# Two stacked convolutions on one core: nine slots for x, and the second convolution's border products behind all its bands

## The reference

```
def _gn(v, G=32, eps=1e-05):           # mean and variance over 3 channels x 128 x 128, per image
    ...
x = x + _L0_conv_ref(_gn(x), w1, w3, w5, alpha)   # alpha0*g + alpha1*dw1(g) + alpha2*dw3(g) + alpha3*dw5(g), depthwise
x = x + _L1_conv_ref(_gn(x), w, b)                # one 3x3 kernel for all channels, plus a bias
```

## Time and profile before

| | us |
|---|---|
| median of 3 runs | 429.32 |
| lowest, highest | 427.31, 429.94 |
| the profiled execution | 432.64 |
| its span | 430.8 |
| busy: PE, DVE, ACT, POOL | 318.5, 318.1, 304.1, 262.3 |

### The profile page before, as it was taken

One profiled execution on the slowest core, in us unless ns is written; L12 is line 12 of the kernel. 1 busy time (PEld: TensorE's weight loads), 2 busy tenths in 40 slices (PEclk: granted clock), 3 DMA queues, 4 the chain that ended last, 5 costly groups with the idle time before them and its releaser, 6 DMA issues.

```text
span 430.8 us, 12547 instructions
## 1 busy us (share of the span) xinstructions
PE 318.5 (74%) x5206; PEld 276.8 (64%) x5206; DVE 318.1 (74%) x688; ACT 304.1 (71%) x372; POOL 262.3 (61%) x206
## 2 busy tenths in 40 slices
PE   2491586754986998679894998499848989898440
PEld 2361273643986798459883897389836989897220
DVE  7861899971886998399929994889649996779620
ACT  1407257089999699939995899759993999977320
POOL 6405055058788578827885588738882788865601
PEclk9997596995999899969996999889998999999685
DMA  6689488201687769676986788676868514731965
GB/s 151 169 174 204 129 188 169 73 3 41 159 200 164 199 177 210 158 189 202 199 194 171 198 184 202 161 214 173 189 163 223 145 41 118 201 97 28 264 173 146
DMA packets 112829, 69.40 MB, mean 161 GB/s; under 512 B 4540, under 2 KB 109892, under 8 KB 112772
## 3 DMA queue, kind: packets, MB, share of 16 engines
q1 hardware_dynamic: 106088, 65.31, 60.5%
q10 hardware_dynamic: 6684, 3.29, 3.3%
HBM read 41.10 MB, written 27.48 MB: 159 GB/s over the span
## 4 chain that ended last, share of the span: by engine, by line
DVE 33%; DMA 21%; SPq 13%; ACT 13%; PE 9%; issue 4%; ACTq 2%; POOL 2%; POOLq 0%; DVEq 0%
DVE xt L697 15%; DVE stats L641 13%; DMA xt<-in_x_dram 10%; PE ps L377 8%; DMA edge_scratch<-gnX 6%; ACT gn_f L551 5%; SPq L236 5%; ACT gnX L552 4%; ACT cross L561 3%; SPq L216 3%; DMA edge_scratch<-gnY 2%; SPq L250 2%; POOL gnX L864 1%; SPq L263 1%; ACTq L244 1%
## 5 line engine op out<-in xcount | busy, mean ns | idle before, releaser
L377 PE MATMUL ps<-gnX,band 64*64 64x512 f16 x2880 | 181.6, 397 | 29.9 <-DVE xt L697 18.1
L377 PEld LDWEIGHTS ps<-gnX,band 64*64 64x64 f16 x2880 | 161.1, 188 | 46.6 <-issue 40.2
L697 DVE SCALAR_TENSOR_TENSOR xt<-ps,unscale,xt 128x512 f32<-128x512 f32 (+1 forms) x194 | 143.8, 747 | 22.9 <-PE ps L377 20.1
L641 DVE BATCH_NORM_STATS2 stats<-xt 128x6 f32<-128x384 f32 x256 | 120.9, 546 | 45.6 <-DMA xt<-in_x_dram 44.9
L377 PE MATMUL ps<-gnY,band 64*64 64x512 f16 x1728 | 116.8, 414 | 33.7 <-DVE xt L697 33.7
L864 POOL TENSOR_TENSOR gnX<-gn_f,gnX 128x768 f16<-128x768 f32 x60 | 92.7, 1545 | 60.7 <-ACT gnX L552 60.7
L377 PEld LDWEIGHTS ps<-gnY,band 64*64 64x64 f16 x1728 | 97.9, 190 | 49.1 <-ACT gnY L552 23.0
L551 ACT ACTIVATE gn_f<-xt,g_add,g_mul 128x768 f32<-128x768 f32 x120 | 122.1, 1017 | 4.9 <-DVE g_add L681 4.3
L864 POOL TENSOR_TENSOR gnY<-gn_f,gnY 128x768 f16<-128x768 f32 x60 | 92.7, 1545 | 31.0 <-ACT gnY L552 31.0
L561 ACT ACTIVATE cross<-ps,unscale 64x512 f32<-64x512 f32 x94 | 64.2, 683 | 51.0 <-PE ps L377 49.4
L873 POOL TENSOR_TENSOR xt<-xt,cross 128x512 f32<-128x512 f32 x47 | 61.7, 1315 | 57.3 <-ACT cross L561 57.2
(11 more groups left out here) (78 smaller groups left out, 97.9 us busy)
## 6 DMA issues: line engine op xcount, KB each, us to landing
out_dram<-xt SPq DMA_DIRECT2D x56, 384.0 KB, 4.8
xt<-in_x_dram SPq DMA_DIRECT2D x48, 384.0 KB, 6.4
band<-diag_scratch SPq DMA_DIRECT2D x48, 160.0 KB, 3.0
haloX<-edge_scratch SPq DMA_DIRECT2D x32, 123.4 KB
xt<-in_x_dram SPq DMA_DIRECT2D x20, 192.0 KB, 4.3
xt<-in_x_dram ACTq DMA_DIRECT2D x12, 192.0 KB, 6.0
out_dram<-xt SPq DMA_DIRECT2D x12, 192.0 KB, 4.0
haloX<-edge_scratch SPq DMA_DIRECT2D x32, 61.7 KB
```

Of the source, the lines that this page charges most:

```text
L377: mm = nc.tensor.matmul(ps[to, c, half, :], weights(rows, half), moving(rows, half), start=first, stop=last)
L641: st = nc.vector.bn_stats(stats[:, q_of(at, i) % 2, at, b, e, :], flat[:, SUB * e:SUB * (e + 1)])
L697: ev = nc.vector.scalar_tensor_tensor(out=here, in0=ps[frm, c, half, :].rearrange("h (b w) -> h b w", b=NB), scalar=unscale[rows, at:at + ...
```

## The change

`xt` gets nine slots of one unit. The channels of a unit are chosen so that two units that follow each other still lie side by side in DRAM; when they do in `xt` too (`joint`), one transfer per image and half moves both, as before. `in_and_out` now stores in odd periods and loads in even ones (the first pair in period 1). `cross` has two slots used in turn in place of one per channel. The weights of X's border products overlap in `halo_wX` (66 columns apart, not 128). TensorE does the bands of all three channels of Y ahead of its border products. The diff, cut to its core (renamed calls of the same meaning and semaphore counts are left out):

```diff
-    NX = 4
+    NX = 9
+    PRE = 4
...
-        halo_w = [sb("halo_wX", [P, NU * CG, 2, R], fp16), sb("halo_wY", [P, 2, R], fp16)]
+        halo_w = [sb("halo_wX", [P, NU * CG * (R + FAR[0]) + R - FAR[0]], fp16), sb("halo_wY", [P, 2, R], fp16)]
...
-        xt = sb("xt", [P, NX, NB, 2, CG, 2, W])
+        xt = sb("xt", [P, NB, NX, CG, 2, W])
...
-        cross = sb("cross", [P, NCROSS, NB, W])
+        cross = sb("cross", [P, 2, NB, W])
...
-            return 4 * CG * (i // 2) + 2 * CG * g + CG * (i % 2)
+            return C // 2 * g + CG * i
...
+        def joint(n):
+
+            return n % NX + 1 < NX
...
+            def stores_in(j):
+
+                if j < LAG + 1:
+                    return None
+                if j == LAG + 1 or j >= NU:
+                    return j - LAG - 1, 1
+                return (j - LAG - 2, 2) if j % 2 else None
+
+            def loads_in(j):
+
+                if j == 1:
+                    return PRE
+                return j + PRE if j % 2 == 0 and 2 <= j < NU - PRE else None
...
             def in_and_out(j, batches):
 
-                m = (j + 3) // 2 if j % 2 else j // 2 - LAG
                 for b in batches:
-                    if j % 2 and 2 <= m < NU // 2:
-                        if m >= NX:
-                            sp.wait_ge(stored[m % NX], 128 * (m // NX))
-                        load_pair(sp, m, b)
-                    elif j % 2 == 0 and m >= 0:
-                        unit_ready(2 * m + 1)
-                        store_pair(sp, m, b)
-                    elif j == PERIODS - 1:
-                        unit_ready(LAST - 1)
-                        store_unit(sp, LAST - 1, b)
+                    if stores_in(j) is not None:
+                        n, units = stores_in(j)
+                        unit_ready(n + units - 1)
+                        store(sp, n, b, units)
+                    n = loads_in(j)
+                    if n is not None:
+                        if n + 1 >= NX:
+                            sp.wait_ge(stored[b], 32 * stores_until(n + 1 - NX))
+                        if joint(n):
+                            load(sp, n, b, 2, x_in[n // 2 % 2])
+                        else:
+                            for k in range(n, n + 2):
+                                load(sp, k, b, 1, x_in[n // 2 % 2])
...
                 if i >= LAG:
                     conv(Y, i - LAG, 0, None, i + 2 if i == LAG or i == NU else None, 0, 5)
                     conv(Y, i - LAG, 1)
-                    if i - LAG < LAST:
-                        edge(Y, i - LAG, 0)
                     conv(Y, i - LAG, 2)
-                    if i - LAG == LAST:
-                        edge(Y, i - LAG, 0)
-                    edge(Y, i - LAG, 1)
-                    edge(Y, i - LAG, 2)
+                    for c in range(CG):
+                        edge(Y, i - LAG, c)
...
-                if i >= 1:
-                    act.wait_ge(cross_added, NCROSS * (i - 1) + min(c, NCROSS - 1) + 1)
+                k = crosses_before(i, c)
+                if k >= 2:
+                    act.wait_ge(cross_added, k - 1)
```

More of the change, by code:

```diff
@@ L133, in preact_conv_stack @@
         x_unit_in = [sem(f"x_unit_in{n}") for n in range(1, 4)]
-        x_in = [sem(f"x_in{r}") for r in range(NX)]
+        x_in = [sem(f"x_in{r}") for r in range(2)]
         band_in = [sem(f"band_in{p}") for p in range(2)]
-        stored = [sem(f"stored{r}") for r in range(NX)]
+        stored = [sem(f"stored{b}") for b in range(NB)]
         edges_landed = [sem(f"edges_landed{s}") for s in "XY"]
@@ L193, in crossed_to, with crosses_before @@
             return sum(crossed(n, c) for n in range(i + 1) for c in range(CG))
+        def crosses_before(i, c):
+            return crossed_to(i - 1) + sum(crossed(i, k) for k in range(c))
         def halo_landed(n):
@@ L239, in edges_in, with images, rows_of, loaded @@
                        .then_inc(halo_in[s][p], 16)
-        def load_unit(eng, n, b, done):
+        def images(t, n, g, b, units):
+            c = first_channel(n, g)
+            return t[b, c:c + units * CG, :, :].rearrange("c (e p) w -> p (c e) w", e=2)
+        def rows_of(n, g, b, units):
+            at = n % NX
+            return xt[HALVES[g], b, at:at + units, :, :, :].rearrange("p u c e w -> p (u c e) w")
+        def joint(n):
+            return n % NX + 1 < NX
+        def loaded(n):
+            return sum(128 if joint(k) else 256 for k in range(PRE, n + 1, 2) if (k - n) % 4 == 0)
+        def load(eng, n, b, units, done):
             for g in range(2):
[L243 to L247, removed]
+                eng.dma_start(rows_of(n, g, b, units), images(x, n, g, b, units)).then_inc(done, 16)
+        def store(eng, n, b, units):
             for g in range(2):
[L249 to L265, removed]
+                eng.dma_start(images(out, n, g, b, units), rows_of(n, g, b, units)).then_inc(stored[b], 16)
         @block.sync
@@ L276, in _ @@
             for b in range(2, NB):
-                load_unit(sp, 0, b, x_first_in[b])
+                load(sp, 0, b, 1, x_first_in[b])
             def save_runs(rows, to, done):
@@ L311, in _ @@
             for b in range(NB):
-                load_unit(sp, 1, b, x_unit_in[0])
+                load(sp, 1, b, 1, x_unit_in[0])
             edges_out(sp, X, 0)
@@ L323, in _ @@
             for b in range(NB):
-                load_unit(sp, 3, b, x_unit_in[2])
+                load(sp, 3, b, 1, x_unit_in[2])
             def unit_ready(n):
@@ L329, in unit_ready, with stores_until @@
                 sp.wait_ge(cross_added, crossed_to(n))
+            def stores_in(j):
[8 more added lines that the diff above has]
+                return j + PRE if j % 2 == 0 and 2 <= j < NU - PRE else None
+            def stores_until(n):
+                return sum(stores_in(j) is not None and sum(stores_in(j)) <= n + 1 for j in range(PERIODS))
             def in_and_out(j, batches):
[L333 removed]
                 for b in batches:
[L335 to L344 removed]
+                    if stores_in(j) is not None:
[11 more added lines that the diff above has]
+                                load(sp, k, b, 1, x_in[n // 2 % 2])
             for j in range(PERIODS):
@@ L364, in _ @@
             for b in (0, 1):
-                store_unit(sp, LAST, b)
-            for r in range(NX):
-                sp.wait_ge(stored[r], 256 if r < NX - 1 else 384)
+                store(sp, LAST, b, 1)
+            for b in range(NB):
+                sp.wait_ge(stored[b], 32 * (stores_until(LAST) + 1))
         @block.tensor
@@ L523, in _ @@
             for b in range(2):
-                load_unit(act, 0, b, x_first_in[b])
+                load(act, 0, b, 1, x_first_in[b])
             act.wait_ge(const_ready, 3)
@@ L582, in _ @@
             for b in range(NB):
-                load_unit(act, 2, b, x_unit_in[1])
+                load(act, 2, b, 1, x_unit_in[1])
             root(1)
@@ L613, in _ @@
             for b in (2, 3):
-                store_unit(act, LAST, b)
+                store(act, LAST, b, 1)
         @block.vector
@@ L869, in cross_add @@
             def cross_add(i, c):
-                pool.wait_ge(cross_out, crossed_to(i - 1) + sum(crossed(i, k) for k in range(c + 1)))
+                k = crosses_before(i, c)
+                pool.wait_ge(cross_out, k + 1)
                 here = x_of(i)[:, :, c, 1, :]
-                nc.gpsimd.tensor_tensor(here, here, cross[:, c, :, :], ALU.add).then_inc(cross_added, 1)
+                nc.gpsimd.tensor_tensor(here, here, cross[:, k % 2, :, :], ALU.add).then_inc(cross_added, 1)
             mid = diag[:, R - 1 - PAD:R + PAD, :][:, ::-1, :]
```

17 lines of the change are left out of this document (9 added, 8 removed).

## The result

The changed kernel takes **450.04 us** (median of 4, 447.00 to 452.16) against 428.31 us for the kernel before on the same chip. The ratio is 1.0503, with an interval of 1.0424 to 1.0583: 5% slower, where 425.6 us was forecast and 436 was the upper end of the range. The profiled execution took 452.16 us, its span is 450.4 us. Some executions of a kernel fall into a slower state, and the ratios here leave those out, so a ratio need not be the quotient of the two medians beside it.

The account below looks back on a forecast made before the run. SP's queue of loads, stores and border transfers was taken as the bound. −3.9 (body) − 1.2 (start) + 1.4 (end) = −3.7 us gave 428.9 in the profile's frame, 425.6 us as a median; range 414 to 436.

Parts of the forecast that it names:

- SP's length: SP's load and store halves 3 to 10: extra load issues add 1 us, four saves of diagonals 3 us.
- half 11: A half runs between two starts of SP's load-or-store block; this one was to start at 300.1, from 296.14.
- What bounds the kernel: Whole loop: SP's full queue sets the pace, 45.4 to 45.9 us a pair of halves; VectorE's stall is its visible end.
- rival 1: Whole loop: engines set the pace, all 34.7 us of VectorE's waits for x go; median 395 us, chance 0.07.
- The body: Loop up to unit 12's evacuation: waits for X's borders replace VectorE's 34.7 us stall, gaining only 3.9 us.
- relief by draining: Saves behind stores: the delay lets queued bytes drain, shortening the next block, so half of their 1.57 us each was taken.
- From unit 12 on: Late loop, no loads left: periods between evacuations were to be 19.25 us both before and after the change.
- TensorE's order: Y's border products behind all Y bands: taken to cost 0, other end +1.2 us for ScalarE's crossing in three late periods.
- The start: Zeroing of halo_wX ahead of VectorE's work on the kernels: 1.38 us in place of 2.62, so −1.2 us.
- The end: Eight stores ahead of unit 14's Y borders: +3.7 us, less 2.3 for faster landing with fewer queued bytes; together +1.4.
- Rival 3: SP's halves and the end: every added instruction counts, start gains nothing; slower, median 437 us, chance 0.20.
- None of the four: The rivals: engines set the pace (395 us, 0.07), added work hidden (418, 0.22), every instruction counts (437, 0.20), nothing (429, 0.10).

Follow-up runs that it names:

- run 5: Changed kernel with 98 unused columns at the end of halo_wX, so that xt starts on a multiple of 512 bytes: 421.13 us, 0.9803.
- run 4: Changed kernel with SP's saves of diagonals moved from store halves to load halves: 444.91 us, 1.0306.
- run 12: Changed kernel with xt aligned and saves in load halves, keeping its new TensorE order: 419.21 us, 0.9755.
- run 7: Changed kernel with xt aligned, saves in load halves and the old TensorE order: 416.22 us, 0.9712.
- run 2: Kernel before with only the new TensorE order, Y's border products behind the bands of all three channels: 435.64 us, 1.0109.
- run 3: Changed kernel with TensorE's old order of Y's border products: 449.66 us, 1.0412.
- run 8: As run 7, with the stores of units 11 and 12 behind the borders of Y of unit 14: 419.15 us, 0.9779.
- run 6: Kernel before with 320 unused bytes ahead of xt, which then starts 64 over a multiple of 256: 452.57 us, 1.0542.
- run 9: Kernel before with 256 unused bytes ahead of xt: 429.84 us, 0.9978.
- run 10: Kernel before with 128 unused bytes ahead of xt: 441.73 us, 1.0288.
- run 11: Kernel before with 320 unused bytes behind xt, so xt stays and the tiles behind it move: 430.31 us, 1.0024.

## Why the prediction was wrong

**The step that failed** is in "SP's length": the block of loads and borders takes 10.4 us "because of the bytes queued (205.24 to 215.68), and the bytes are the same". The bytes were the same and the packets weren't: 37.8 ns each in place of 33.9. The block itself grew only from 10.4 to 11.1 us, but the same assumption stands behind every other length and landing that the sum carried over. The change to halo_wX was priced by its memset alone (−1.2), but it also set where xt begins. I had asked what the smaller tile itself costs, and not what lies behind it. In numbers: 450.04 against 421.13 with xt aligned, and 452.57 against 429.42 in the kernel before. The misplacement costs 23 us there and nearly 29 here, which is more than the whole loss. In the sum, half 11 was due at 298.9 (300.1 less the start's 1.2) and came at 320.06, +21.2; from there to the start of half 15 (due at 374.2, which is 379.3 less 3.9 and 1.2; it came at 401.34) 6.0 us more were lost; the end gave back 3.9. Together 23.3, the distance of 450.4 from the forecast span of 427.1. Against the same kernel aligned (run 5) the changed one is 11.9 us late at half 5 (163.90 for 152.04) and 26.0 at half 11 (320.06 for 294.10).

**What bounds the kernel: right.** SP and its transfers make up 67% of the chain; in the middle SP waits for no engine to speak of; rival 1 (engines set the pace, 395 us) is out in every run. That fits a price of 11% on a packet and 5% on the time.

**The body, right once its packets are.** "Not −34.7" and the exchange of the stall for haloX waits hold in both versions: 36.8 us as changed, 24.3 us aligned. Evacuations in the middle came 23.8 to 27.3 us apart as changed, where 22 to 24 was forecast. With xt aligned, halves 5 to 11 take 142.06 us, 4.3 more than before, where saves and extra issues were put at 4.0. The split was off: of the 16 loads in half 4 no share falls in those halves, and three saves do, each at its full 1.6 us in a store half (runs 4 and 12); no relief by draining shows. Unit 12 is evacuated at 312.01 in run 5 (316.7 was forecast with the start), 17.9 us after half 11 began, where 17.8 was taken; in the changed kernel at 339.00, 18.9 after.

**From unit 12 on, wrong by little.** Periods were to be 19.25; as changed they are 21.5 (339.00 to 360.51) and then 20.9, 3.9 of the 6.0 us above. The last wait for haloX ends at 338.22, so slow packets aren't what stretches them: TensorE waits 3.0 us for VectorE in the two and is busy for 20.3 and 19.2 us, at a mean granted clock of 0.92 of full speed, a mix of its two levels, 2.4 and 1.2 GHz. Ahead of the first it had stood 5.4 us for haloX. In the kernel before, the last two such periods had a clock of 1.00, 2.4 GHz throughout, and 17.9 and 17.7 us of work (the one ahead of them, after a stall, took 19.15 at 0.91, with 15.8 us of work in it). Run 5 has 19.6 us at 1.00 and then 20.8 at 0.92; run 7 has 20.9 at 0.87, then 19.3 and 19.2 at 1.00. So these periods go with the granted clock, which the forecast took to stay as it was; why it fell where it did stays open.

**TensorE's order: wrong** in the kernel before: +1.1%, some 4.7 us, where 0 was taken with +1.2 as the other end (run 2). The path over ScalarE to SP's border write was missed. In the changed kernels it is hidden or too small to tell (runs 3 and 12).

**The start.** VectorE's rows of the changed kernel:

```profile
2.66 1.40 DVE L656 MEMSET halo_wX<- 128x1615 uint32 x1 [0.29 <-issue]
...
4.37 0.34 DVE L774 TENSOR_SCALAR kern<-k_w,k_alpha 97x25 f32<-97x25 f32 x1
...
42.67 3.78 DVE L666 BATCH_NORM_STATS2 stats<-xt 128x6 f32<-128x384 f32 x8 [9.30 <-DMA xt<-in_x_dram]
```

The memset takes 1.40 us (1.38 forecast) and the work on the kernels begins 1.4 us sooner (4.37; 5.74 in the trace before), so the test that I named, a start near 5.5, comes out in its favour. SP's save follows, 7.27 for 8.53. But the 9.30 us wait for unit 2's x stays as it was (9.03), and the gain is gone by SP's loads at 34.10 (33.12 before); half 1 begins at 57.10, 4.1 us later than before. With xt aligned the same row reads

```profile
33.93 3.78 DVE L666 BATCH_NORM_STATS2 stats<-xt 128x6 f32<-128x384 f32 x8 [0.36 <-DMA xt<-in_x_dram]
```

half 1 begins at 50.08 (52.98 before), and half 5 starts 6.3 us earlier than before, where 1.2 was forecast for all of it. This wait is at most 3.1 us in the four aligned versions of the changed kernel (runs 5, 7, 8, 12) and 7.9 to 10.5 us in every other run, so it takes the alignment together with something else of the change; what that is was not separated.

**The end.** SP's and ScalarE's rows answer to the earlier trace rows:

```profile
401.34 11.27 SPq L270 DMA_DIRECT2D out_dram<-xt  x8
412.70 2.50 SPq L225 DMA_DIRECT2D edge_scratch<-gnY  x2
416.83 2.61 SPq L241 DMA_DIRECT2D haloY<-edge_scratch  x4
```

```profile
422.07 3.50 ACT L585 ACTIVATE cross<-ps,unscale 64x512 f32<-64x512 f32 x5 [2.23 <-PE ps L402]
```

The last one is of the chain of waits, and answers to the earlier trace rows:

```profile
426.13 2.66 DMA edge_scratch<-gnY
```

The eight stores take 11.27 us (10.7 forecast), the crossing follows 20.7 us after the half's start (23.0 forecast), and ScalarE's last borders land in 2.66 us where it was 4.45: 1.8 us of the relief that I put at 2.3. That it comes from fewer bytes in the queue was not tested. From the crossing to the end it is 28.3 us, 32.2 before. The end was costed 3.9 us too high.

**Luck.** Run 5, the change without the misplacement, has a span of 419.0 us where 427.1 was forecast, and this nearness is partly luck: half 11 comes 4.8 us earlier than forecast by way of the start, from there to half 15 (372.38) it is 3.0 us more, and the end is 6.3 us shorter.

**The rivals.** Rival 3 had the direction and a share of the cause, the saves at full price, but priced the whole at 437, and its mark, half 11 after 304, was passed by 16 us for another reason. None of the four had a transfer that takes longer for the same bytes. What I named as proof against the forecast, pairs past 48 us, is what happened.

**What the page on DMA says.** The traces show a price at 64 and 128 over a multiple of 256 and none at 256. The Trainium skill, page "DMA: Bandwidth & Descriptors", section "How a descriptor splits into AXI transactions", has a reason that would fit: a transfer that doesn't start on a 256-byte boundary begins at the boundary below, and the bytes before its start cost beats (32 bytes each) too. By that count, an estimate from the page's rule, a 512-byte packet needs 16 beats when aligned, 18 at 64 over, and 20 at 128 over. For 64 over the trace is near it: +12.5% in beats, and 33.9 to 37.8 ns, +11%. For 128 over it isn't: +25% in beats against 37.2 ns, +10%, and half the loss of time. The page speaks of bytes that are fetched, and here the loads, which write to SBUF, pay too (landing 6.4 to 7.2 us). The measurement decides: a start off a multiple of 256 costs 3.3 and 3.9 ns a packet in the two cases tried. That the starting address is the cause is shown by runs 5, 6, 9, 10 and 11; that extra beats are the way it acts is not, and why the kernel loses less at 128 than at 64, at nearly the same mean packet, stays open.

The other figure of the Trainium skill that the prediction names (same page, "Anatomy of one DMA", 5.6 us) is a fit to DMAs issued from GpSimd, and SP issues these. The row of 10.4 us decides.

## What to carry to other kernels

When an edit changes the size of any tile, look where the tiles behind it now start; a tile whose rows travel in 512-byte packets did best here beginning on a multiple of 256 bytes, and a strip of unused columns is the cheapest edit in this study. "The same bytes" is no proof of the same transfer time: compare the queue's share of engine time at equal bytes, and when all transfers are slower by a like factor, think of addresses before order. And when a producer's order changes, follow each consumer in the order of its own engine to the engine that sets the pace, also where no one waits today.

## What the runs showed of the hardware

- A 512-byte packet between DRAM and SBUF takes 32.9 to 34.0 ns in the mean of a run when its SBUF start is on a multiple of 256 bytes, 37.2 at 128 over one and 37.8 to 38.4 at 64 over. In the kernel before, landings of 384 KB transfers go from 6.4 us (loads) and 4.8 (stores) to 6.7 and 5.0 at 128 over and to 7.2 and 5.2 at 64 over, and the kernel's time grows by 2.9% and 5.4%.
- Whether the two channel groups of a unit lie 6 or 48 channels apart in DRAM costs nothing (run 1, 0.9952), nor does moving the tiles behind xt by 320 bytes (run 11, 1.0024).
- The delay shows again in the small transfers queued behind those of x: with 9.6% more engine time, border writes behind loads land in 5.9 (X) and 7.1 us (Y) in place of 4.9 and 6.3, and a pair of halves grows by 6.1 us, of which only 1.7 is added work.
- In the tail of the loop, with no wait for borders, a period in which TensorE is busy for 17.7 to 18.2 us at a granted clock of 1.00 takes 19.2 to 19.8 us (before, runs 5, 7 and 12); one with 19.1 to 20.3 us of work at 0.92 takes 20.8 to 21.5 (the changed kernel and run 5).
